# The out-projection of an attention kernel, made for four heads at a time instead of sixteen

## The reference

```python
q = rope(einsum('bim,ghmd->bghid', x, w_aq)); k = rope(einsum('bim,gmd->bgid', x, w_ak))
v = einsum('bim,gmd->bgid', x, w_av)
p = softmax(causal(einsum('bghid,bgjd->bghij', q * qk_mult, k * qk_mult)))
o = einsum('bghij,bgjd->bghid', p, v)
x = layernorm(x + einsum('bghid,ghdm->bim', o, w_ao))        # the out-projection
x = layernorm(x + routed_experts(x) + shared_expert(x))
```

## Time and profile before

| | |
|---|---|
| median of 3 executions | 1074.61 us (1071.99 to 1074.84) |
| the profiled execution's own time | 1066.11 us |
| its span in the trace | 1064.3 us |
| mean granted TensorE clock | 0.966 of full speed |
| PE busy | 959.4 us, 90% of the span |
| DVE busy | 681.5 us, 64% |
| ACT busy | 487.9 us, 46% |
| POOL busy | 371.4 us, 35% |

### The profile page before, as it was taken

One profiled execution on the slowest core, in us unless ns is written; L12 is line 12 of the kernel. 1 busy time (PEld: TensorE's weight loads), 2 busy tenths in 40 slices (PEclk: granted clock), 3 DMA queues, 4 the chain that ended last, 5 costly groups with the idle time before them and its releaser, 6 DMA issues.

```text
span 1064.3 us, 16754 instructions
## 1 busy us (share of the span) xinstructions
PE 959.4 (90%) x5240; PEld 735.6 (69%) x5240; DVE 681.5 (64%) x1703; ACT 487.9 (46%) x1083; POOL 371.4 (35%) x334
## 2 busy tenths in 40 slices
PE   8999988989999999999979999999999998569744
PEld 6888866667787777776766667878777776445411
DVE  5988953775767675757656667585857656424326
ACT  4112124555656464645545456564645645135402
POOL 3878873234323111011154232303021211136811
PEclk9999998999999999999989999999999999879868
DMA  8786775563222111111243234351211123988687
GB/s 242 235 282 213 261 247 159 152 166 108 75 66 60 61 50 61 46 31 53 77 127 96 68 100 129 87 143 40 76 36 60 47 55 98 266 235 197 86 287 279
DMA packets 137303, 137.24 MB, mean 129 GB/s; under 512 B 18065, under 2 KB 108805, under 8 KB 137216
## 3 DMA queue, kind: packets, MB, share of 16 engines
q1 hardware_dynamic: 84064, 98.33, 30.1%
q10 hardware_dynamic: 43872, 29.50, 9.4%
q0 software_dynamic: 9280, 8.34, 4.3%
HBM read 86.44 MB, written 63.05 MB: 140 GB/s over the span
## 4 chain that ended last, share of the span: by engine, by line
PE 66%; DVE 11%; issue 8%; DMA 6%; SPq 3%; POOL 2%; ACT 2%; ACTq 1%; POOLq 0%; DVEq 0%
PE s_ps L1119 14%; PE ring L1129 9%; PE o_ps L1149 8%; PE ring L1158 8%; PE o_ps L1146 7%; PE s_ps L1098 6%; PE ring L1098 5%; DVE neg_max L1322 2%; SPq L762 2%; DMA sums<-erow,goal_u 2%; PE o_ps L1098 2%; DMA inverses<-inv_t 1%; PE s_ps L1122 1%; PE s_ps L1212 1%; POOL slot_rows L849 1%
## 5 line engine op out<-in xcount | busy, mean ns | idle before, releaser
L1322 DVE TENSOR_REDUCE neg_max<-s_ps 128x1 f32<-128x128 f32 (+7 forms) x256 | 191.5, 751 | 137.7 <-PE s_ps L1122 136.1
L964 ACT ACTIVATE probs<-s_ps,neg_max 128x128 f32<-128x128 f32 (+7 forms) x256 | 189.7, 741 | 139.1 <-DVE neg_max L1322 131.2
L1119 PE MATMUL s_ps<-kt,qt_hi 128*128 128x512 f32 (+3 forms) x768 | 234.3, 387 | 5.8 <-ACT probs L964 3.7
L827 POOL TENSOR_TENSOR qt_lo<-q_raw,qt_hi 128x512 fp32r<-128x512 f32 x64 | 82.0, 1283 | 320.3 <-ACT qt_hi L878 320.1
L1129 PE MATMUL ring<-ident,probs 128*128 128x128 f32 x1152 | 176.7, 276 | 10.1 <-DVE pt_lo L1256 5.2
L878 ACT ACTIVATE pt_hi<-ring 128x512 fp32r<-128x512 f32 x168 | 99.9, 596 | 181.5 <-PE ring L1129 179.8
L1119 PEld LDWEIGHTS s_ps<-kt,qt_hi 128*128 128x128 f32 x768 | 139.4, 194 | 53.5 <-issue 29.5
L1256 DVE TENSOR_TENSOR pt_lo<-ring,pt_hi 128x512 fp32r<-128x512 f32 x168 | 115.6, 688 | 60.2 <-ACT pt_hi L878 58.4
L1129 PEld LDWEIGHTS ring<-ident,probs 128*128 128x128 f32 x1152 | 128.6, 142 | 34.6 <-issue 15.5
L1149 PE MATMUL o_ps<-pt_hi,v 128*128 128x512 f32 x336 | 146.2, 436 | 0.9 <-DVE pt_lo L1256 0.9
L1119 PE MATMUL s_ps<-kt,qt_lo 128*128 128x512 f32 (+3 forms) x384 | 134.2, 350 | 0.0
(11 more groups left out here) (201 smaller groups left out, 1373.6 us busy)
## 6 DMA issues: line engine op xcount, KB each, us to landing
qk_rows<-prods SPq DMA_DIRECT2D x80, 256.0 KB, 3.0
q_raw<-qk_rows ACTq DMA_DIRECT2D x128, 128.0 KB, 2.9
inv_row<-inverses SPq DMA_DIRECT2D x64, 256.0 KB, 3.5
fsum<-sums SPq DMA_DIRECT2D x48, 256.0 KB, 7.9
sums<-blank SPq DMA_DIRECT2D x16, 640.0 KB, 4.9
wexp<-in_L_ffn_w_gate_dram SPq DMA_DIRECT2D x32, 192.0 KB, 4.1
wexp<-in_L_ffn_w_up_dram SPq DMA_DIRECT2D x32, 192.0 KB, 4.7
wexp<-in_L_ffn_w_down_dram SPq DMA_DIRECT2D x32, 192.0 KB, 5.8
```

The source lines that it names most:

```text
L964: act.activation(probs[:, u % 2, h, 0:blocks(u) * P], s_ps[:, n % 2, score_cols(n)], ACT.Exp, bias=neg_max[:, n % 8:n % 8 + 1], accum_out= ...
L1119: pe.matmul(s_ps[:, n % 2, c + a:c + e], q[qp], k[kp][:, a:e], start=(qp == kp == 0), stop=(qp == 1 and not last))
L1322: dve.tensor_reduce(neg_max[:, n % 8:n % 8 + 1], s_ps[:, n % 2, score_cols(n)], AX_X, ALU.max, negate=True).then_inc(max_ready, 1)
```

## The change

`outproj` becomes a step of a unit: 4 matmuls over the unit's four heads into a bank of their own, so 64 steps of 4 in place of 16 steps of 16. `yadd` becomes a step of a unit too: the first adds the bank to the residual, the others add their bank to `y_sb`, and the layer norm's statistics follow the last. The new function `outward()`, called by `product()`, puts the first three units' steps into the list as soon as `omul` is three `pv` back (two in tiles with one or two key blocks), and their `yadd` one `pv` later. The last unit of a tile keeps the old place of BETWEEN. Each step takes a turn of the three banks, so there are 48 more turns and the banks behind them move. `fit` stands a head earlier in tiles 0 and 8, the four loads of the weights `wo` are issued from other places by POOL, and `omul` waits for the unit's own part of the out-projection four units back, where it waited for the whole tile before.

```diff
--- before.py
+++ after.py
@@ -94,7 +94,7 @@
     (("pick", 6), -2, (1, 3, 3, 0)),
     (("pick", 7), -2, (1, 3, 3, 1)),
     (("count",), -2, (2, 4, 4, 2)),
-    (("fit",), -2, (3, 5, 5, 2)),
+    (("fit",), -2, (2, 5, 5, 2)),
     (("place",), -2, (4, 5, 5, 4)),
     (("scat", 0), -2, (5, 6, 6, 5)),
     (("outproj",), -1, (6, 7, 6, 6)),
@@ -120,6 +120,9 @@
 ]
 
 
+OF_LAST_GROUP = ("outproj", "yadd")
+
+
 def projections():
 
     seq = [("xt", i) for i in range(CHUNK)] + [("projv", i) for i in range(CHUNK)]
@@ -143,6 +146,7 @@
 
 
 KSPLIT_AT = [14, 16, 18, 20]
+WO_AT = [("exp", 1, 1), ("exp", 1, 3), ("exp", 2, 0), ("exp", 2, 2)]
 K_LOAD_AT = [(8, 2), (9, 2), (10, 2), (11, 2)]
 BLANK_AT = [(c, name, 0, 1) for c in range(CHUNKS) for name in (0, 2)]
 
@@ -156,13 +160,27 @@
 
 
 
-    seq, waiting = [], []
+    seq, waiting, normed = [], [], []
+
+    def outward(ahead):
+
+        for unit in list(normed):
+            u, age, steps = unit
+            unit[1] = age + ahead
+            while steps and steps[0][1] <= unit[1]:
+                seq.append((steps.pop(0)[0], u))
+            if not steps:
+                normed.remove(unit)
 
     def product():
+        outward(1)
         u, j = waiting.pop(0)
         seq.append(("pv", u, j))
         if j == blocks(u) - 1:
             seq.append(("omul", u))
+            if u % G < G - 1:
+                at = 3 if blocks(u) > 2 else 2
+                normed.append([u, 0, [("outproj", at), ("yadd", at + 1)]])
             if 0 <= u - NT * G + 1 < G:
                 seq.append(("vsplit", u - NT * G + 1))
 
@@ -182,13 +200,15 @@
 
     def misc(i, at):
 
-        out = []
         for step, ahead, heads in BETWEEN:
             tile = i + ahead
             if heads[min(i % NT, len(heads) - 1)] != at or not 0 <= tile < TILES:
                 continue
-            out.append((step[0], tile) + step[1:])
-        return out
+            if step[0] in OF_LAST_GROUP:
+                outward(UNITS)
+                seq.append((step[0], tile * G + G - 1))
+                continue
+            seq.append((step[0], tile) + step[1:])
 
     late = H + 1
     for n in range(HEADS):
@@ -210,7 +230,7 @@
             drain(i * G)
         if h == 1 and u in KSPLIT_AT:
             seq.append(("ksplit", 1, KSPLIT_AT.index(u)))
-        seq += misc(i, n % (G * H))
+        misc(i, n % (G * H))
     p = TILES - 1
     seq += [("pick", p - 1, 6), ("pick", p - 1, 7), ("count", p - 1), ("fit", p - 1), ("place", p - 1)]
     seq += [("scat", p - 1, n) for n in range(3)]
@@ -218,7 +238,9 @@
         for _ in lagging(m):
             pass
     drain(UNITS)
-    seq += [(s, p) for s in ("outproj", "yadd", "norm", "x1t", "x1lo", "rtr", "sig")] + [("pick", p, n) for n in range(8)]
+    outward(UNITS)
+    seq += [(s, UNITS - 1) for s in OF_LAST_GROUP]
+    seq += [(s, p) for s in ("norm", "x1t", "x1lo", "rtr", "sig")] + [("pick", p, n) for n in range(8)]
     seq += [("count", p), ("fit", p), ("place", p)] + [("scat", p, n) for n in range(3)]
     seq += [(s, p) for s in ("shared", "ht", "htlo", "sd", "zadd")]
     return seq
@@ -738,7 +760,7 @@
 
                     sp.wait_ge(pv_done, PT_AT[(UNITS - 2, blocks(UNITS - 2) - 1)] + 1)
                     load_homes(kt[0], v_sb[0], kt[1], *[v[:, 0, :, :, :]] * (G - 1))
-                if s == ("outproj", TILES - 1):
+                if s == ("outproj", UNITS - 1):
 
                     sp.wait_ge(pv_done, PT_ALL)
                     load_homes(kt[0], v_sb[0], kt[1], v, q_raw, qt_hi, qt_lo, probs, pt_hi, pt_lo, most=BEFORE_ROUTING)
@@ -746,7 +768,7 @@
                     i = s[1]
                     read(sp, ("sd", i))
                     sp.dma_start(sums[i * P:(i + 1) * P, :], z_sb[:, :]).then_inc(z_stored, 16)
-            sp.wait_ge(attn_ready, TILES)
+            sp.wait_ge(attn_ready, UNITS)
             sp.wait_ge(srow_loaded[1], 16)
             load_homes(kt[0], v_sb[0], kt[1], v, q_raw, qt_hi, qt_lo, probs, pt_hi, pt_lo, ot)
             sp.wait_ge(z_stored, 16 * TILES)
@@ -831,11 +853,11 @@
                     pool.wait_ge(v_later_hi, g + 1)
                     pool.tensor_tensor(v[:, g, 1, :, :], v[:, g, 1, :, :].bitcast(F32), v[:, g, 0, :, :].bitcast(F32),
                                        ALU.subtract).then_inc(v_later, 1)
-                if s[0] == "yadd":
-                    pool.wait_ge(var_ready, s[1] + 1)
+                if s[0] == "yadd" and s[1] % G == G - 1:
+                    pool.wait_ge(var_ready, s[1] // G + 1)
                     pool.tensor_tensor(rstd[:, :], var_eps[:, :], minus_half[:, :], ALU.pow).then_inc(rstd_ready, 1)
-                if s[0] == "exp" and 1 <= s[1] <= G and s[2] == 1:
-                    g = s[1] - 1
+                if s in WO_AT:
+                    g = WO_AT.index(s)
                     pool.wait_ge(proj_ready, PROJ_ALL)
                     pool.dma_start(wo[:, g * H:(g + 1) * H, :], w_ao[g].rearrange("h d m -> d h m")
                                    ).then_inc(wo_loaded, 16)
@@ -1150,13 +1172,12 @@
                                             start=False, stop=(last and vp == 1))
                     ins.then_inc(pv_done, 1)
                 if kind == "outproj":
-                    i = s[1]
+                    u = s[1]
                     pe.wait_ge(wo_loaded, 16 * G)
-                    for h in range(G * H):
-                        if h % H == 0:
-                            pe.wait_ge(o_ready, G * i + h // H + 1)
-                        ins = pe.matmul(bank(s)[:, 0:M], ot[:, h // H, (h % H) * P:(h % H + 1) * P], wo[:, h, :],
-                                        start=(h == 0), stop=(h == G * H - 1))
+                    pe.wait_ge(o_ready, u + 1)
+                    for h in range(H):
+                        ins = pe.matmul(bank(s)[:, 0:M], ot[:, u % G, h * P:(h + 1) * P], wo[:, u % G * H + h, :],
+                                        start=(h == 0), stop=(h == H - 1))
                     ins.then_inc(attn_ready, 1)
                 if kind == "x1t":
                     i = s[1]
@@ -1336,20 +1357,25 @@
                     i, g = divmod(u, G)
                     dve.wait_ge(inv_loaded[u % 2], 16 * (u // 2 + 1))
                     dve.wait_ge(pv_done, PT_AT[(u, blocks(u) - 1)] + 1)
-                    if i >= 1:
-                        dve.wait_ge(attn_ready, i)
+                    used(dve, attn_ready, u - G + 1)
                     if u == 0:
                         dve.wait_ge(v_stored, 16 * VS)
-                    dve.tensor_tensor(ot[:, g, :], o_ps[:, :], inv_row[:, u % 2, :], ALU.mult).then_inc(o_ready, 1)
+                    dve.tensor_tensor(ot[:, u % G, :], o_ps[:, :], inv_row[:, u % 2, :], ALU.mult).then_inc(o_ready, 1)
                 if kind == "yadd":
-                    i, s = s[1], ("outproj", s[1])
-                    dve.wait_ge(attn_ready, i + 1)
-                    if i == 0:
+                    u, s = s[1], ("outproj", s[1])
+                    i, g = divmod(u, G)
+                    dve.wait_ge(attn_ready, u + 1)
+                    if u == 0:
                         dve.wait_ge(wo_loaded, 16 * G)
                     n = TILES + i
-                    dve.wait_ge(x_loaded[n % XB], 16 * (n // XB + 1))
-                    reader(dve.tensor_tensor(y_sb[:, :], bank(s)[:, 0:M], x_sb[:, n % XB, :], ALU.add), s)
+                    if g == 0:
+                        dve.wait_ge(x_loaded[n % XB], 16 * (n // XB + 1))
+                    else:
+                        read(dve, ("outproj", u - 1))
+                    reader(dve.tensor_tensor(y_sb[:, :], bank(s)[:, 0:M], y_sb[:, :] if g else x_sb[:, n % XB, :],
+                                             ALU.add), s)
                     read(dve, s)
+                if kind == "yadd" and u % G == G - 1:
                     after(dve.bn_stats(stats[:, :], y_sb[:, :]))
                     after(dve.bn_aggr(mean_var[:, :], stats[:, :]))
                     dve.tensor_scalar(var_eps[:, :], mean_var[:, 1:2], EPS, None, ALU.add).then_inc(var_ready, 1)
```

## The result

The change made the kernel slower. The changed kernel ran at 1079.24 us (median of 7, 1076.21 to 1082.51), the kernel before, timed beside it, at 1072.88 (median of 7). The medians are 6.4 us apart; the ratio taken over the executions is 1.0072, with a 95% interval of 1.0045 to 1.0098, so about 7.7 us more, and between 4.8 and 10.5. I had forecast 1072, some 2.5 us less. The profiled execution took 1076.21 us, its span is 1074.4.

A forecast was written before the change was run, and what follows sets the result against it. PE, busy 90% of the span, was taken to bound the kernel. −10.9 + 6.0 + 1.4 + 1.0 = −2.5 us against the profiled 1066.1 gave 1063.6, or 1072 as a median; the range was 1065 to 1081.

The forecast's parts named there:

- The matmuls themselves: PE's out-projection matmuls: none removed, each four-head part 1.73 us, the split costed at 0, with 0 to +2 for the range.
- What the moved parts fill: PE's waits for pt_lo, ot, chose and ht_lo, filled by early parts: 12.1 us, nine tenths taken, 10.9 saved.
- The `ht_lo` waits: Two PE waits for ht_lo behind places that get a part, counted as filled: 1.6 us with the correction.
- the `ot` wait at 562.26: PE's wait of 0.51 us for ot at a unit's turn; a part in front fills it, counted as 0.7.
- rival 2: Filled waits come back, since DVE sets the pt_lo waits: +2.4 us, 1077, no change to be told; chance 0.15.
- The last quarter: Last unit's matmuls wait uncovered for its omul in tiles 1, 2, 7, 9, 10, 15: six times 1.0, 6.0 us.
- unit 61's `ot`: Trace example pricing an exposed omul: 1.09 us from the end of the last pv to PE's next product.
- The adds: 48 more DVE adds, 20.0 us, fit in DVE's slack; PE loses 1.4 us where a bank's turn comes too early.
- the four that I named: Bank turns too early in tiles 2 and 10 (shared expert), 3 and 11 (first unit's add), 0.3 to 0.4 us each.
- Behind attention: Expert weight load released by the last pv meets the last tile's scatter: 1.0 us, bounds 0 to 3.
- Rival 3: Slower: adds in DVE's queue hold banks ahead of results PE needs, 0.6 us each; at 16 places +5.7, 1080; chance 0.17.
- Rival 4: Slower: exposed omuls make PE's clock fall, 3.3 us a stretch; two make +4.1, 1079; chance 0.06.

The follow-up runs named there:

- e11: Changed kernel with each early add right behind its part, last eight heads in one step, early parts one product later; 1063.60 us, ratio 0.9942 to before.
- e4: The kernel before with only the side edits: fit a head earlier in tiles 0 and 8, wo loads issued from the new places; 1073.81 us, ratio 1.0011.
- e5: Changed kernel with each early add listed right behind its out-projection instead of one product later; 1073.56 us, ratio 1.0028 to before.
- e6: Changed kernel with the second and third groups' adds cut to 8 of 256 columns, in the same places; 1079.14 us, ratio 1.0075 to before.
- e8: Changed kernel, early parts only in tiles 5, 6, 13, 14 (first four heads) and 7, 15 (two parts), otherwise one step; 1064.82 us, ratio 0.9947 to before.
- e10: Like e8, early parts only in tiles 5, 6, 7, 13, 14, 15, but each early add right behind its out-projection; 1062.91 us, ratio 0.9919 to before.

## Why the prediction was wrong

The sum was −10.9 + 6.0 + 1.4 + 1.0. Step by step:

- **The matmuls themselves**, 0: right. A part takes 1.73 us start to start where an fp32 product follows (204.63 to 206.36 in tile 1, and in e11 the same from 200.46 to 202.19), 1.54 where one in two parts (`pt_hi`, `pt_lo`) or scores follow; before, the 16 matmuls took 6.72. I had named a change of PE's busy time of over 5 us at the same clock as a sign against the mechanism. It rose by 5.9 us, but at a clock of 0.961 against 0.966, and in e4, which leaves the out-projection as it was, it is 966.5 us at 0.956. So it says nothing here.
- **What the moved parts fill**, 10.9: too high by 3.3. (I counted ten waits for `pt_lo`; there are nine, 0.2 us less.) Filled were 3.7 in tiles 5, 6, 13, 14, about 2.8 in tile 7, 0.6 in tile 15 and 0.5 before `chose`, together 7.6. The `ht_lo` waits, 1.6 in my list, became `pt_lo` waits of about the same size, and the `ot` wait at 562.26 one for `ahead`. A wait that DVE's backlog makes is not filled when the part in front of it brings the next DVE result nearer. This was the mechanism of rival 2 at work, in tiles 3, 8 and 11. Tile 0's share can't be told: with nearly the same order there it took 23.1 to 26.9 us.
- **The last quarter**, 6.0: right, six waits, 0.93 in the bracket and 1.1 start to start at five of them, 6.6. The price from unit 61's `ot` held.
- **The adds**, 1.4: this is the step that failed, by 7.5 us, which alone turns the sign. "Following the turns of the three banks through the new list I find about four places … 0.3 to 0.4 us each" should have been ten, of 0.6 to 1.6: 8.9 us in the balance above. At the four that I named no wait for an add appeared; the ten are others, in tiles 1, 2, 4 and 5 and their like in the second sequence. I took the price from the old waits for `y_sb`, but an early add doesn't stand where the old one stood: it is queued behind an `omul`, row maxima and the choosing of experts. And I looked for banks that an add frees late, not for banks that a part takes early; the waits for `hid` and for `ht_lo` are such. e5 shows the first kind (4.3 us by moving the adds), e11 the second (neither wait is left in tiles 1, 2, 9 and 10). 0.6 us a place, my upper price, was also too low for tiles 1 and 9.
- **Behind attention**, 1.0: can't be told. From the first `omul` of tile 15 to PE's restart on the scattered rows were 72.4 us before, 73.4 after, and 75.2 in e4 without the change.

With the measured sizes the sum is −7.6 + 6.6 + 8.9 = +7.9; the ratio says +7.7. That they agree so well is in part luck: the sum leaves out tile 0 and all behind attention, and the interval is 4.8 to 10.5. Rival 3 had the sign and nearly the size (+5.7, 1080), for the reason that an add holds a bank, and its sign came true: the waits for `y_sb` and `pt_lo` are 8.1 us, over 5. It counted late adds of one price; e6 shows that the middle ones' length doesn't matter. I gave it 0.17, since DVE's share was 68%: a share says nothing of where in the queue an add stands, and in tile 1 DVE was even idle with the add's input ready.

Rival 4 is out: the granted clock is 1.00 in 190 to 240, 240 to 355 and 600 to 735, where four of the stands for `ot` lie, and 1.00 over the whole of 190 to 540: the fall that I had named as its sign didn't come.

The `y_sb` adds kept 412 ns in the mean, with the bank and one SBUF input, where `row` took 710:

```profile
L1387 DVE TENSOR_SCALAR row<-y_sb,mean_var,rstd 128x256 f32<-128x256 f32 x16 | 11.4, 710 | 1.2 <-POOL rstd L858 1.1
...
L1375 DVE TENSOR_TENSOR y_sb<-ring,y_sb 128x256 f32<-128x256 f32 x48 | 19.8, 412 | 6.5 <-PE ring L1179 6.5
```

In the kernel before none of the 16 adds ran beside an instruction of POOL, so my "beside a POOL that is often busy" had no row behind it. In the changed kernel 22 of the 64 do, by POOL's spans, which are rough, and none takes over 426 ns. The rule of the Trainium skill (SBUF — State Buffer, "Who interferes with whom"), that a DVE instruction with at most one SBUF input doesn't contend with GpSimd, agrees with these 22. The Trainium skill says so, in that section, for instructions outside DVE's two-port modes, a condition that I had left out. The row write too reads one SBUF tensor, yet beside POOL it takes from 404 to 1357 ns, and 413 and 414 the two times it runs alone; in which mode it runs no row here shows.

## What to carry to other kernels

Splitting a step that uses a shared ring of buffers costs turns, not work: for each new turn look up who last read that buffer and where the reader of the new one stands in its engine's queue, for every tile shape, before counting what the split fills. Put the reader right behind its producer. And when parts move ahead, keep one part, not the last, between the last producer and what waits for it. If the last part moves back instead, everything that hangs on it, here its add and the layer norm, has to be looked up again.

## What I had not expected of the hardware

The clock can spare a fall for no reason that I see in the trace. In tile 7 PE waits 1.76 us for `row` in both e8 and e10, which differ only in the place of the early adds. In e10, as before, the granted clock is 0.66 over 540 to 550; in e8 it is 1.00, and tile 7 is 56.48 us long instead of 59.03. This is one execution of each. The two stretches, e8 and then e10, in the columns of the earlier trace rows:

```profile
540.00:550.00 10.00, 4.61 (x34) 3.94 (x35) 7.27 (x19) 5.19 (x18) 7.68 (x7) 1.00 0.67 176
```

```profile
540.00:550.00 10.00, 7.60 (x34) 6.39 (x34) 4.80 (x15) 4.45 (x16) 6.14 (x6) 0.66 0.60 161
```

And the stage ahead of attention, the same in all kernels but for the places of the loads of `wo`, ended, counted to the first `omul`, between 165.6 and 172.0 us. That is 0.6% of the time by itself; it is why I read tiles and not spans.
